# Turning normed tiles into columns on DVE, in strips of 32x32 squares over two slots, in place of four transposes on PE

## What is computed

```python
x = x + tanh(g_xattn) * attention(layernorm(x), ctx, mask, bias, Wq, Wk, Wv, Wo)   # 32 heads of 128
x = x + tanh(g_ffn) * (layernorm(x) @ W.T + bias + lora(layernorm(x)))              # 3 adapters of rank 16
```

## Time and profile before

| what | value |
|---|---|
| median of 3 runs | 1740.77 us (1740.27 to 1741.35) |
| the profiled execution | 1740.83 us |
| its span | 1739.0 us |
| PE busy | 1721.0 us, 8634 matmuls |
| DVE busy | 1153.3 us, 2521 instructions |
| ACT busy | 696.6 us, 1481 instructions |
| POOL busy | 792.9 us, 1067 instructions |
| granted clock of TensorE, mean | 0.998 of full speed |

### The profile page before, as it was taken

The page is one execution under the profiler, slowest core; times in us unless marked ns, Lnnn a source line. Parts: engine busy times, 40 slices in busy tenths (PEclk is TensorE's granted clock), DMA queues, the critical chain, the costliest instruction groups (busy, mean ns, idle before and its releaser), DMA issues.

```text
span 1739.0 us, 25524 instructions
## 1 busy us (share of the span) xinstructions
PE 1721.0 (99%) x8634; PEld 1460.0 (84%) x8634; DVE 1153.3 (66%) x2521; ACT 696.6 (40%) x1481; POOL 792.9 (46%) x1067
## 2 busy tenths in 40 slices
PE   8999999999999999999999999999999999999998
PEld 7788888888888888888888888888888888888887
DVE  5677667777676665666666666566666766666664
ACT  5555555554333442343333343233433333333331
POOL 5667766775344432344344343334443443333431
PEclk9999999999999999999999999999999999999999
DMA  7777777766445444545445454355454454454431
GB/s 277 267 261 264 269 269 267 281 248 218 180 170 200 170 169 157 189 176 196 167 168 195 167 190 177 135 201 192 164 182 181 170 188 170 160 191 164 171 127 55
DMA packets 111524, 336.63 MB, mean 194 GB/s; under 512 B 13377, under 2 KB 13505, under 8 KB 111394
## 3 DMA queue, kind: packets, MB, share of 16 engines
q1 hardware_dynamic: 111250, 334.73, 54.5%
q10 hardware_dynamic: 144, 0.26, 0.1%
HBM read 263.64 MB, written 71.30 MB: 193 GB/s over the span
## 4 chain that ended last, share of the span: by engine, by line
PE 94%; DVE 2%; issue 1%; DMA 1%; ACT 1%; POOL 1%; SPq 0%; ACTq 0%; DVEq 0%
PE vo_bank L309 13%; PE vo_bank L311 13%; PE vo_bank L310 13%; PE q_bank L309 7%; PE q_bank L311 7%; PE q_bank L310 7%; PE k_bank L309 6%; PE k_bank L311 6%; PE k_bank L310 6%; PE pv_two L314 5%; PE s_two L314 5%; PE s_two L315 2%; PE pv_two L315 2%; PE vo_bank L590 1%; DVE score L950 0%
## 5 line engine op out<-in xcount | busy, mean ns | idle before, releaser
L1197 POOL TENSOR_TENSOR score<-score,row_max 128x256 f32<-128x256 f32 x128 | 78.9, 616 | 683.7 <-DVE row_max L955 683.6
L1132 POOL TENSOR_TENSOR ot_lo<-attn,ot_hi 128x512 fp32r<-128x512 f32 x128 | 166.1, 1298 | 149.0 <-ACT ot_hi L696 149.0
L309 PE MATMUL q_bank<-xt_hi,wq 128*128 128x512 f32 x512 | 208.6, 407 | 0.0
L768 ACT ACTIVATE attn<-pv_two 128x512 f32<-128x512 f32 x128 | 76.7, 599 | 316.9 <-PE pv_two L315 316.9
L311 PE MATMUL q_bank<-xt_hi,wq 128*128 128x512 f32 x512 | 200.7, 392 | 0.0
L310 PE MATMUL q_bank<-xt_lo,wq 128*128 128x512 f32 x512 | 200.1, 391 | 0.0
L309 PE MATMUL k_bank<-ct_hi,wk 128*128 128x512 f32 x512 | 199.5, 390 | 0.2 <-DVE ct_lo L888 0.2
L950 DVE SCALAR_TENSOR_TENSOR score<-s_two,raw_bias 64x256 f32<-64x256 f32 x256 | 107.8, 421 | 138.2 <-PE s_two L315 135.9
L310 PE MATMUL k_bank<-ct_lo,wk 128*128 128x512 f32 x512 | 199.4, 389 | 0.0
L311 PE MATMUL k_bank<-ct_hi,wk 128*128 128x512 f32 x512 | 199.3, 389 | 0.0
L309 PE MATMUL vo_bank<-wv,ct_hi 128*128 128x512 f32 x504 | 196.2, 389 | 0.0
(11 more groups left out here) (196 smaller groups left out, 3835.2 us busy)
## 6 DMA issues: line engine op xcount, KB each, us to landing
wv<-wv_split SPq DMA_DIRECT2D x96, 512.0 KB, 5.3
wq<-wq_split SPq DMA_DIRECT2D x96, 512.0 KB, 3.2
wk<-wk_split SPq DMA_DIRECT2D x96, 512.0 KB, 3.6
wo<-wo_split SPq DMA_DIRECT2D x96, 512.0 KB, 5.2
raw_bias<-in_pair_bias SPq DMA_DIRECT2D x64, 256.0 KB, 5.8
wq_split<-wq SPq DMA_DIRECT2D x32, 512.0 KB, 2.9
wk_split<-wk SPq DMA_DIRECT2D x32, 512.0 KB, 4.1
wv_split<-wv SPq DMA_DIRECT2D x32, 512.0 KB, 5.9
```

The costliest lines, as they stand in the source:

```text
L309: pe.matmul(to, left[0], right[0], start=first, stop=False)
L768: act.activation(by(attn, PB), pv_two[:, :, 1, :], ACT.Copy).then_inc(ot_b, 1)
L1132: pool.tensor_tensor(to, src, f32(of), ALU.subtract).then_inc(done, 1)
L1197: pool.tensor_tensor(score[:, :, :], score[:, :, :], row_max[:, :].unsqueeze(2).to_broadcast([P, PB, S]), ALU.subtract).then_inc(shift_don ...
```

## The change

The 24 tiles turned in the loop are no longer turned by PE. DVE turns them with its own transpose of 32x32 squares: 16 instructions per tile, each taking a strip of 32 rows and one column block of 32 out of each of the four chunks of 128 columns (32 partitions x 4 x 32 elements), out of xn and into a new SBUF buffer xn_cols at another group of 32 partitions. Eight of them (`away` 0 and 1) stand at the end of the tile's slot behind `row_scales`, eight (`away` 2 and 3) at the end of the next slot. ACT's copy and DVE's subtraction follow two slots after the tile's slot (`turned_at`), with xn_cols as their source. The turns are no longer among the jobs of the vo banks. `LEAD_TURNS` becomes 24, 25, 28, 29; `LORA` becomes 15 and 18; `DENSE` becomes 16, 17, 19, 20. The first and last four tiles stay on PE.

```diff
--- before.py
+++ after.py
@@ -42,8 +42,8 @@
 LEAD, FFN = 0, 1
 
 
-FFN_SUMS, FFN_PIECES, FFN_TURNS, LORA, DENSE = (5, 6), (7, 8, 11, 12), (9, 10, 13, 14), (15, 16), (17, 18, 19, 20)
-X_LOAD, LEAD_SUMS, LEAD_PIECES, LEAD_TURNS = 21, (22, 25), (23, 24, 27, 28), (25, 26, 29, 30)
+FFN_SUMS, FFN_PIECES, FFN_TURNS, LORA, DENSE = (5, 6), (7, 8, 11, 12), (9, 10, 13, 14), (15, 18), (16, 17, 19, 20)
+X_LOAD, LEAD_SUMS, LEAD_PIECES, LEAD_TURNS = 21, (22, 25), (23, 24, 27, 28), (24, 25, 28, 29)
 CONSTANTS, LORA_LOAD, LORA_PIECES = (6, 7, 8, 9, 10), 11, (13, 14)
 WARM_UP = 10
 
@@ -56,6 +56,11 @@
     if n < SLOTS and b < BLOCKS - 1 and s in LEAD_TURNS:
         return LEAD, b + 1, LEAD_TURNS.index(s)
     return None
+
+
+def turned_at(n):
+
+    return turn_at(n - 2)
 
 
 def sums_at(n):
@@ -124,8 +129,6 @@
         found += [("v", values_at(n)[0], t) for t in values_at(n)[1]]
     if output_at(n):
         found += [("o", output_at(n)[0], t) for t in output_at(n)[1]]
-    if turn_at(n):
-        found += [("turn", *turn_at(n))]
     if lora_at(n):
         found += [("lora", *lora_at(n))]
     if dense_at(n):
@@ -151,13 +154,14 @@
     PLACE["lora", END, _p] = f"pv{_p}"
 USED_LAST, EMPTIED, TURNED = {}, {}, {}
 _count = {"act": 0, "dve": 0}
+LOOP_TURNS = [("turn", *turn_at(n)) for n in range(SLOTS) if turn_at(n)]
 for _i, _j in enumerate(ALL_JOBS):
     USED_LAST[_j] = next((j for j in reversed(ALL_JOBS[:_i]) if PLACE[j] == PLACE[_j]), None)
     _who = "act" if _j[0] == "v" else "dve"
     _count[_who] += 1
     EMPTIED[_j] = _who, _count[_who]
-    if _j[0] == "turn":
-        TURNED[_j] = len(TURNED) + 1
+for _i, _j in enumerate([j for j in FIRST_JOBS if j[0] == "turn"] + LOOP_TURNS + [j for j in LAST_JOBS if j[0] == "turn"]):
+    TURNED[_j] = _i + 1
 V_BLOCKS = 6
 
 
@@ -225,6 +229,7 @@
 
         stage = [sb(f"stage{i}", [P, 512]) for i in range(2)]
         xn = [sb(f"xn{i}", [P, D]) for i in range(2)]
+        xn_cols = [sb(f"xn_cols{i}", [P, C, P]) for i in range(2)]
         lo_t = two("lora", [P, 2, PAIR])
         stats = sb("stats", [P, PB, 6])
         mean_var = sb("mean_var", [P, PB, 2])
@@ -264,6 +269,7 @@
             sem(f"{m}_lo") for m in ("q", "k", "v", "pt", "ot", "wq", "wk", "wv", "wo", "stage", "lead_ct", "lora"))
         wq_saved, wk_saved, wv_saved, wo_saved, wq_back, wk_back, wv_back, wo_back = (
             sem(f"w{m}_{w}") for w in ("saved", "back") for m in "qkvo")
+        strip_done, turn_lo = sem("strip_done"), sem("turn_lo")
         vo_free, v_free, ot_b, ot_sum, acc_done = sem("vo_free"), sem("v_free"), sem("ot_b"), sem("ot_sum"), sem("acc_done")
         gate_done, exp_done, var_done, pow_done, bias_done = (
             sem(f"{m}_done") for m in ("gate", "exp", "var", "pow", "bias"))
@@ -294,6 +300,13 @@
             if job is not None:
                 who, count = EMPTIED[job]
                 eng.wait_ge(v_free if who == "act" else vo_free, count)
+
+        def turned_cols(eng, job):
+
+            if job in LOOP_TURNS:
+                eng.wait_ge(turn_lo, LOOP_TURNS.index(job) + 1)
+            else:
+                emptied(eng, job)
 
         def wait(eng, done, count):
             if count > 0:
@@ -482,7 +495,7 @@
             def queries(n):
                 b = n // H
                 if n % H == 0:
-                    emptied(pe, ("turn", LEAD, b, PB - 1))
+                    turned_cols(pe, ("turn", LEAD, b, PB - 1))
                 if n < H:
                     pe.wait_ge(wq_lo, n + 1)
                 else:
@@ -593,7 +606,7 @@
             def lora_inner(b, p):
                 job = ("lora", b, p)
                 emptied(pe, USED_LAST[job])
-                emptied(pe, ("turn", FFN, b, 2 * p + 1))
+                turned_cols(pe, ("turn", FFN, b, 2 * p + 1))
                 if b == 0:
                     pe.wait_ge(stage_lo, 4)
                 for c in range(C):
@@ -627,8 +640,6 @@
                 keys(n)
                 main_job(n, 0)
                 main_job(n, 1)
-                if turn_at(n):
-                    turn(*turn_at(n))
                 if lora_at(n):
                     lora_inner(*lora_at(n))
                 if dense_at(n):
@@ -780,8 +791,12 @@
 
             def turn(norm, b, t):
                 job = ("turn", norm, b, t)
-                act.wait_ge(vo_ps, NUMBER[job] + 1)
-                hi(xt[b % 2][0][:, :, cols(t, P)], by(bank_of(job), C), turn_hi)
+                if job in LOOP_TURNS:
+                    act.wait_ge(strip_done, 4 * (LOOP_TURNS.index(job) + 1))
+                    hi(xt[b % 2][0][:, :, cols(t, P)], xn_cols[t % 2][:, :, :], turn_hi)
+                else:
+                    act.wait_ge(vo_ps, NUMBER[job] + 1)
+                    hi(xt[b % 2][0][:, :, cols(t, P)], by(bank_of(job), C), turn_hi)
 
             def piece(n):
                 z, what, c = piece_at(n)
@@ -822,8 +837,8 @@
                 if n > 0:
                     main_job(n, 0)
                     main_job(n, 1)
-                if turn_at(n):
-                    turn(*turn_at(n))
+                if turned_at(n):
+                    turn(*turned_at(n))
                 if lora_at(n):
                     lora(*lora_at(n))
                 if n > 0:
@@ -979,18 +994,35 @@
             def normalise(norm, b, t):
                 r = run(norm, b)
                 dve.wait_ge(rstd_done, 2 * r + t // 2 + 1)
-                if t >= 2:
-                    dve.wait_ge(vo_ps, NUMBER["turn", norm, b, t - 2] + 1)
-                elif r > 0:
-                    before = [job for job in ALL_JOBS if job[0] == "turn" and run(job[1], job[2]) == r - 1]
-                    dve.wait_ge(vo_ps, NUMBER[before[t + 2]] + 1)
+                ahead = [job for job in TURNED if run(job[1], job[2]) == (r if t >= 2 else r - 1)]
+                if ahead:
+                    job = ahead[t - 2]
+                    if job in LOOP_TURNS:
+                        dve.wait_ge(strip_done, 4 * (LOOP_TURNS.index(job) + 1))
+                    else:
+                        dve.wait_ge(vo_ps, NUMBER[job] + 1)
                 dve.tensor_scalar(xn[t % 2][:, :], acc[b % 2][:, t, :], mean_var[:, t, 0:1], rstd[:, t:t + 1],
                                   ALU.subtract, ALU.mult).then_inc(xn_done, 1)
 
             def turn(norm, b, t):
                 job, at = ("turn", norm, b, t), (slice(None), slice(None), cols(t, P))
                 dve.wait_ge(turn_hi, TURNED[job])
-                lo(xt[b % 2][1][at], by(bank_of(job), C), xt[b % 2][0][at], vo_free)
+                if job in LOOP_TURNS:
+                    lo(xt[b % 2][1][at], xn_cols[t % 2][:, :, :], xt[b % 2][0][at], turn_lo)
+                else:
+                    lo(xt[b % 2][1][at], by(bank_of(job), C), xt[b % 2][0][at], vo_free)
+
+            def strips(norm, b, t, late):
+
+                z = LOOP_TURNS.index(("turn", norm, b, t))
+                src, to = by(xn[t % 2], C), xn_cols[t % 2]
+                dve.wait_ge(xn_done, PB * run(norm, b) + t + 1)
+                wait(dve, turn_lo, z - 1)
+                for away in ((2, 3) if late else (0, 1)):
+                    for i in range(C):
+                        j = (i + away) % C
+                        last = dve.transpose(to[cols(j, S // 2), :, cols(i, S // 2)], src[cols(i, S // 2), :, cols(j, S // 2)])
+                    last.then_inc(strip_done, 1)
 
             def lora_gate(b, p):
                 job, rows = ("lora", b, p), slice(0, STACK)
@@ -1066,6 +1098,10 @@
                 if lora_at(n):
                     lora_rest(*lora_at(n))
                 row_scales(n)
+                if turn_at(n - 1):
+                    strips(*turn_at(n - 1), True)
+                if turn_at(n):
+                    strips(*turn_at(n), False)
                 if n in CONSTANTS:
                     constants(CONSTANTS.index(n))
```

## The result

| what | before | after |
|---|---|---|
| median | 1740.87 us (4 runs, 1740.27 to 1741.35) | 1759.67 us (4 runs, 1756.57 to 1761.34) |
| ratio to before | | 1.0106, 95% interval 1.0089 to 1.0124 |
| the profiled execution | 1740.83 us, span 1739.0 | 1756.57 us, span 1754.8 |
| granted clock, mean of the profiled one | 0.998 | 0.996 |

The change makes the kernel slower by 1.1%, clearly more than the 0.2% that can be told.

What follows compares the result with a forecast made beforehand. TensorE (PE), busy 99% of the span, was taken as the bound. New PE waits of 30.7 us against 16 removed gave +15 on 1740.8, so 1755 us, range 1735 to 1768.

Steps and rivals of the forecast that it cites:

- Removed, 16.2 us: On PE's queue: 10.8 us of 96 turning matmuls and 5.4 us of waits for a bank go.
- A strip's pitch, 0.333: On DVE: each of 384 strips takes 0.333 us, as from SBUF to PSUM, adding 128 us.
- My upper bound of 0.38: On DVE: strip pitch of 0.38 us if strips now and then meet POOL, judged from xn's durations.
- the rival of shorter strips: On DVE: at 0.285 us pitch waits equal the removed 16 us; at 0.27, 1736 us; chance of faster 0.20.
- The reserve, twelve fit and sixteen do not: In a slot: 2.12 us free between reciprocal and prob's transposes (T); sixteen strips end kt 1.25 us late.
- Lateness handed on: From slot to slot: DVE's lateness at a slot's end carries on; an FFN run gets 4.4 us of PE waits.
- LEAD runs: Slots 25 to 31: new PE waits of 5.3 us per run, 6.9 in block 0 with its weight subtractions.
- The clock falls: Behind three to six long PE waits the clock falls, costing 8 to 17 us: 1763 to 1772; chance 0.12.
- LoRA and dense moved, no price: Slots 16 to 18: same matmuls, sum unchanged; if a bank is not free, up to 0.7 us times three.
- Signs of being wrong: Strips at 0.27 us or less, slots 11 and 26 at 12.76, waits at q_bank or vo_bank, clock 0.50 behind slot 26.

Runs made afterwards that it cites:

- the runs with twelve and eight strips: Changed kernel with the last four, or half, of each tile's sixteen strips left out, so twelve or at most eight stand behind one slot: 1736.37 us and 1732.28 us.
- the moved statistics: Changed kernel with the second LEAD statistics moved from slot 25 to slot 23, nothing else: 1753.40 us, ratio 1.0072.
- The run with early copies: Changed kernel with ACT's copy and DVE's subtraction of the turned tile moved ahead of the slot's main jobs: 1759.17 us, ratio 1.0106.
- the run with the filled wait: Changed kernel with eight extra matmuls ahead of the scores in slot 26 of blocks 0 to 2, inside PE's wait: 1758.67 us, ratio 1.0099.
- LoRA's wait: Changed kernel with LoRA's first half in slot 16 instead of 15 and dense in 17, 18, 19, 20: 1758.50 us, ratio 1.0102.
- the last kernel: Changed kernel with turns spread out, copies early, and block 0's four tiles turned by PE in slots 23, 25, 27, 29: 1731.90 us, ratio 0.9943.

## Why the prediction was right

Predicted 1755 with a range from 1735 to 1768, measured 1759.67. The net was put at +15; it is +15.7 between the profiled executions and +18.8 between the medians. The mechanism is the predicted one: sixteen strips behind one slot make kt late, and PE waits in slots 11, 26 and 30 and for the value eviction in slot 15. That the sum of the waits came so close (32.2 us, 30.7 predicted) is in part luck, for terms of opposite sign cancelled: the LEAD runs of blocks 1 and 2 were put 1.8 us too high, that of block 0 3.3 too low, and a wait that was left out in slot 13 made up for others that were too long. The steps:

- *Removed, 16.2 us.* Right. Slots 9, 10, 14 and 25 have their 12.76, and the waits for acc are gone.
- *A strip's pitch, 0.333.* Sixteen take 5.10 us: (5.10 - 0.303) / 15 = 0.320. A strip has a median of 303 ns into SBUF where L930 has 325 into PSUM. The Trainium skill's table (VectorE: DVE Perf Modes, The TRN2 errata) has 58 cycles for SBUF to SBUF and 120 for PSUM to SBUF, and no column for a result in PSUM; I had put the 120 on the destination, which made 65 ns, and the trace shows 22 for that. The 311 ns that the Trainium skill has for a turn (The three transpose paths, on the same page) are for 128x128 in bf16, in 32x32 blocks, and so no price for a float32 strip. My upper bound of 0.38, for strips that meet POOL and grow as xn does, was not reached: in 354 of their 384 places POOL had an instruction under way, and none took over 0.309 us. The measured pitch lies well above the 0.285 at which the change would have broken even. That was the rival of shorter strips.
- *The reserve, twelve fit and sixteen do not.* Right, shown by the runs with twelve and eight strips. At a pitch of 0.320, sixteen strips make T move by 5.13 + 0.72 - 2.12 = 3.7 us.
- *Lateness handed on.* Right, shown by the moved statistics. An FFN run costs 4.4 us as forecast, but by other parts: 1.2 for 1.6 in slot 11, 0.4 for 0.2 in slot 12, 1.8 for 2.5 in slot 15, and 1.05 in slot 13 where I had none. (My parts add up to 4.3, not 4.4.) In slots 11 and 15 the pitch takes off 0.2 us, and the rest is that DVE was not late: in both the reciprocal ends at s+3.46 at the latest, an ordinary slot's s+3.45, where I had it 0.2 and 0.6 later. The one in slot 13 was missed: the first output matmul of slots with n % 4 of 1 starts at s+5.53 where nothing is late, and needs POOL's ot_lo, which then ends at s+4.68. That is a reserve of 0.85 us where kt has 2.7. In slot 13 DVE and behind it POOL are 1.7 us late, ot_lo ends at s+6.39 and the matmul starts at s+6.44: a second way by which DVE's lateness reaches PE.
- *LEAD runs.* 4.4 for 5.3: in slot 26 2.55 for 3.1, by the pitch and a lateness of 1.35 us where I had 1.7, in slot 30 1.3 for 1.6; with 0.36 of slot 31 for the next block's queries, a wait that I had priced at nothing ("the queries of slot 32 for tiles done in 31"). The run with early copies shows it is that. Block 0 cost 10.2 for 6.9: 1.4 us in slot 26 are the clock behind the 3.3 us wait, by the run with the filled wait. The rest was not followed slot by slot; a weight subtraction there takes up to 1.65 us in the longest of its 32 places, and I had counted 0.7.
- *The clock falls.* I gave it 0.12; it happened once in the profiled execution. The mean clock of the four runs was 0.996, 0.995, 0.994 and 0.994 for 1756.57, 1758.93, 1761.34 and 1760.41 us, so the slower runs have more time at the lower level. A fall costs 1.4 us in slot 26 (LoRA's wait, above), so two more of them would make the 3 us between the profiled run and the median, an estimate that stays open: only one of the four has a trace.
- *LoRA and dense moved, no price.* Right to 0.2 us per block.
- *Signs of being wrong.* Two of those named did appear, both small: waits at vo_bank and q_bank (slots 13 and 29, and the start of a block), and a granted clock of 0.50 behind slot 26 of block 0.

## What to carry to other kernels

Work moved off the bounding engine costs nothing only where the receiving engine has idle time between two deadlines, not on the average: here 2.6 us of strips in a slot were free outside block 0, the 3.8 of twelve strips only where DVE was on time, and 5.1 nowhere, and the same 384 instructions gave a loss of 1.1% in neighbouring slots and a gain of 0.5% spread out. Write down, for each result that the bound engine takes from the other, when it is wanted and when it ends; count the second and third reader of a late engine too (here ot_lo by way of POOL, and a bank by way of ACT). Where extra work is put, see that no other extra work makes the engine late just before it.

## What was not expected of the hardware

- A 32x128 float32 transpose on DVE takes 303 ns from SBUF to SBUF and 325 from SBUF to PSUM; a subtraction hardly cares (692 ns from SBUF in the changed kernel, 692 from PSUM).
- Behind one and the same wait of 2.21 us, in slot 26 of blocks 1 and 2, the granted clock stayed at 1.00 both times in the changed kernel, fell to 0.50 both times with LoRA in slot 16, and fell once of two with early copies. In the last kernel it fell behind 2.10 us (slot 23) and not behind 2.13 (slot 27). So the length of the wait alone did not decide here.
- The subtraction into xt_lo, with both sources in SBUF, took 0.69 us in every one of its 24 places in the changed kernel, where POOL was idle beside it. With early copies 8 of the 24 took 1.36, each beside a POOL subtraction into ct_lo for 0.81 us of it, and the median was still 0.69. The one into qt_lo, with a source in PSUM, took at most 0.70 in all of its 128 places, though POOL was working beside it in most.
